# Edge terms of every fourth batch of edge_attr_128 computed in the count stage of the first mean layer instead of in the gated pass

## The reference

```python
x = _layernorm(x + _L0_gnn_ref(x, edge_index, edge_attr_64, ...))   # gated messages
x = _layernorm(x + _L1_gnn_ref(x, ..., src, dst))                   # mean of neighbours
x = _layernorm(x + _L2_gnn_ref(x, edge_index, edge_attr_128, ...))  # two attention layers
x = _layernorm(x + _L3_gnn_ref(x, edge_index, ...))                 # two mean layers
```

## Time and profile before

| | us |
|---|---|
| median of 3 runs | 2037.59 |
| lowest and highest run | 2037.51, 2041.03 |
| the profiled execution | 2039.3 |
| its span, first to last instruction | 2037.5 |
| gated pass, steady part, in the span | 79.41 to 642.36 |
| count stage, pairs 0 to 207 | 683.88 to 962.40 |

### The profile page before, as it was taken

How to read it: one execution, slowest core, us unless ns; L and a number is a source line. 1 busy time by engine, 2 the same in 40 slices (tenths; PEclk the granted TensorE clock), 3 DMA queues, 4 the chain that set the end, 5 groups by cost and what they waited for, 6 DMA issues and landing times. The chain is left out here.

```text
span 2037.5 us, 42968 instructions
## 1 busy us (share of the span) xinstructions
PE 1742.0 (85%) x13651; PEld 1405.7 (69%) x13651; DVE 1412.8 (69%) x4286; ACT 911.7 (45%) x2490; POOL 983.6 (48%) x998
## 2 busy tenths in 40 slices
PE   5799999999999558888466999967599999299996
PEld 5699999999998425445464878757467878166664
DVE  5687788888886778885667766655676664744656
ACT  2566667676665266664303544421154453411100
POOL 3776777777774300000356777735577775300000
PEclk9799999999999759999768999986699999699998
DMA  6988788888884011222352111107221111344542
GB/s 191 269 241 240 235 240 255 256 249 246 255 255 148 7 55 55 109 109 89 127 143 62 45 41 43 45 15 200 70 67 41 41 43 37 123 162 180 198 163 87
DMA packets 145067, 276.87 MB, mean 136 GB/s; under 512 B 28295, under 2 KB 88333, under 8 KB 141556
## 3 DMA queue, kind: packets, MB, share of 16 engines
q1 hardware_dynamic: 104526, 191.58, 29.2%
q0 software_dynamic: 35456, 79.88, 14.5%
q10 hardware_dynamic: 4854, 2.55, 0.5%
HBM read 228.82 MB, written 45.08 MB: 134 GB/s over the span
## 5 line engine op out<-in xcount | busy, mean ns | idle before, releaser
L959 POOL DMA_INDIRECT gated_rows<-p_tab,src_idx x416 | 429.7, 1033 | 176.0 <-issue 104.4
L1351 POOL DMA_INDIRECT ring<-table,src_idx x384 | 384.1, 1000 | 146.4 <-issue 93.0
L2159 PE MATMUL bank<-counts,mean_xs 128*128 128x416 bf16 (+2 forms) x1350 | 219.5, 321 | 32.0 <-DVE mean_xs L1671 32.0
L1000 PE MATMUL bank<-gated_wide_q,gated_comb 128*128 128x256 f32 x832 | 216.8, 384 | 0.0
L1157 DVE TENSOR_TENSOR gated_pre<-bank,gated_rows 128x512 f32<-128x512 f32 x208 | 142.8, 687 | 101.8 <-PE bank L1000 101.8
L2159 PEld LDWEIGHTS bank<-counts,mean_xs 128*128 128x128 bf16 x1350 | 126.2, 98 | 116.1 <-issue 34.4
L1482 ACT COPY attention_counts<-bank 128x475 f32 (+1 forms) x224 | 127.2, 568 | 176.3 <-PE bank L1506 153.4
L1517 PEld LDWEIGHTS bank<-attention_counts,h_sb 128*128 128x128 f32 x900 | 157.5, 190 | 62.3 <-ACT attention_counts L1482 3.8
L1073 ACT ACTIVATE gated_sig<-gated_pre 128x512 f32<-128x512 f32 x208 | 131.1, 630 | 154.1 <-DVE gated_pre L1157 152.0
L1517 PE MATMUL bank<-attention_counts,h_sb 128*128 128x232 f32 (+1 forms) x900 | 191.9, 341 | 2.3 <-DVE attention_counts L1574 1.7
L1506 PE MATMUL bank<-attention_wide_b,scratch 128*128 128x400 f32 x448 | 189.5, 505 | 0.0
(11 more groups left out here) (428 smaller groups left out, 4018.7 us busy)
## 6 DMA issues: line engine op xcount, KB each, us to landing
counts<-count_tabs SPq DMA_DIRECT2D x16, 2675.0 KB, 9.9
h_sb<-in_edge_attr_dram SPq DMA_DIRECT2D x51, 512.0 KB, 4.9
count_tabs<-mean_counts SPq DMA_DIRECT2D x8, 2675.0 KB, 7.8
gated_relr<-rel_rows SPq DMA_DIRECT2D x104, 128.0 KB
gated_ids<-id_rows SPq DMA_DIRECT2D x26, 512.0 KB
gated_wide_q<-q_tab SPq DMA_DIRECT2D x208, 64.0 KB
attend_hot_lo<-low_hots SPq DMA_DIRECT2D x52, 256.0 KB, 3.3
gated_ea<-in_edge_attr_dram SPq DMA_DIRECT2D x51, 256.0 KB
```

The source lines that it names most:

```text
L959: pool.indirect_dma_start(out=rows[:, q % TICKS, c, :], out_offset=None, in_=p_tab, in_offset=bass.IndirectOffsetOnAxis(ap=src_idx[:, b, j ...
L1000: mm = pe.matmul(PRE[q % 2][:, c * 2 * P:(c + 1) * 2 * P], comb[:, u, k, c, :], wide_q[:, u, c, :], start=True, stop=True)
L1351: pool.indirect_dma_start(out=rows[:, n % RING, j, :], out_offset=None, in_=table, in_offset=bass.IndirectOffsetOnAxis(ap=src_idx[:, gathe ...
L2159: mm = pe.matmul(BANKS_D[q % ND][:, 0:width], xs[l][:, m // 3, m % 3, :], counts[:, s % 2, m // 3, at:at + width], start=(m == 0), stop=(m ...
```

## The change

`LEFT` is the set of batches 1, 5, 9, ..., 101 (26 of 104). For these the gated pass no longer loads, turns, copies or multiplies edge_attr_128: `turn_ea` keeps the transpose of edge_attr_64 alone, `turn_silu` keeps silu alone, ACT's L1068 and L1079 fall away. A load of two batches of edge_attr_128 becomes one of one batch where the second is in LEFT; the number of DMAs stays.

In `mean_build` SP loads these batches into six buffers in `scratch` (the first six at the start, the others in between the stores of the tables). At pairs 61, 66, ..., 186 PE turns one batch behind `count(n)` (four transposes into bank TURN), ACT copies it behind `copy_counts(n)` (512 columns), and two pairs later PE multiplies it with `ae_v` behind `count(n+2)` (four matmuls, eight passes, two columns) into bank 7. At pair 190 ACT copies all terms into `ae`. The first turn waits until the W_self products have been taken. Pairs 61 to 186 lie in the third to eighth block. The core of the diff:

```diff
+    LEFT = range(1, NB, UN)
...
-                        for c in range(2):
-                            mm = pe.transpose(EAT[:, (1 + c) * P:(2 + c) * P], ea128[:, u, 2 * k + c, :], ident[:, :])
+                        if by_pe(b):
+                            for c in range(2):
+                                mm = pe.transpose(EAT[:, (1 + c) * P:(2 + c) * P], ea128[:, u, 2 * k + c, :], ident[:, :])
...
-                        for c in range(2):
-                            mm = pe.matmul(ST[:, 2 * (P + c):2 * (P + c) + 2], eaT[:, q % TRN, c, :], ae_v[:, :], start=True, stop=True)
+                        if by_pe(q // PAIRS):
+                            for c in range(2):
+                                mm = pe.matmul(ST[:, 2 * (P + c):2 * (P + c) + 2], eaT[:, q % TRN, c, :], ae_v[:, :], start=True, stop=True)
...
+            EA_FROM, EA_STEP = 2 * SBP + 9, 5
+            EA_AT = {EA_FROM + EA_STEP * i: i for i in range(NE)}
+            TERMS_AT = max(EA_AT) + 4
...
+                    due = [(EA_FROM + EA_STEP * (i - ER + 1), load, i) for i in range(ER, NE)] + [((s + 1) * SBP, keep, s) for s in range(NSB)]
...
+                    def place_eaT(i):
+                        act.wait_ge(ea_turned, i + 1)
+                        reach(act, ea_made, i - 1)
+                        act.copy(flat(eaT[:, i % 2, :, :]), TURN[:, :]).then_inc(eaT_ready, 1)
...
                         copy_counts(n, values)
+                        if n in EA_AT:
+                            place_eaT(EA_AT[n])
...
+                    def turn_ea(i):
+                        pe.wait_ge(ea_in[i % ER], 16 * (i // ER + 1))
+                        reach(pe, eaT_ready, i)
+                        for j in range(J):
+                            mm = pe.transpose(TURN[:, j * P:(j + 1) * P], ea128[:, i % ER, j, :], ident[:, :])
+                        mm.then_inc(ea_turned, 1)
...
+                    def multiply_ea(i):
+                        pe.wait_ge(eaT_ready, i + 1)
...
+                        for j in range(J):
+                            at = 2 * (i * J + j)
+                            mm = pe.matmul(TERMS[:, at:at + 2], eaT[:, i % 2, j, :], ae_v[:, :], start=True, stop=True)
+                        mm.then_inc(ea_made, 1)
...
                             count(n)
...
+                            if n in EA_AT:
...
+                                turn_ea(EA_AT[n])
+                            if n - 2 in EA_AT:
+                                multiply_ea(EA_AT[n - 2])
```

More of the change, by code:

```diff
@@ L161, in build_program @@
     place_a, origin_a = sb("place_a", [1, NSB * ATP], I32), sb("origin_a", [1, LAST], I32)
+    LEFT = range(1, NB, UN)
+    assert NB - 1 not in LEFT and UN == 4
     ae_v, ae = sb("ae_v", [P, 2]), sb("ae", [P, 2, NB, J])
@@ L866, in batch, with by_pe @@
                 return q // PAIRS, q % PAIRS, q // PAIRS % UN
+            def by_pe(b):
+                return b not in LEFT
             def rounds_of(engine):
@@ L1065, in place_eaT @@
                         act.copy(comb[low, u, k, 0, :], EAT[low, 0:P])
-                        act.copy(comb[high, u, k, 1, :], EAT[high, 0:P])
-                        reach(act, s_turned, q - TRN + 1)
-                        act.copy(flat(eaT[:, q % TRN, :, :]), EAT[:, P:3 * P]).then_inc(eaT_ready, 1)
+                        ins = act.copy(comb[high, u, k, 1, :], EAT[high, 0:P])
+                        if by_pe(b):
+                            reach(act, s_turned, q - TRN + 1)
+                            ins = act.copy(flat(eaT[:, q % TRN, :, :]), EAT[:, P:3 * P])
+                        ins.then_inc(eaT_ready, 1)
                     def sigmoid(q):
@@ L1686, in mean_build @@
             most, flag = sb("most", [1, 1]), sb("flag", [1, 1], I32)
+            ea128 = scratch[:, 0:ER * J * P].rearrange("p (b j d) -> p b j d", b=ER, j=J)
+            NE = len(LEFT)
+            eaT = flat(cur[:, :, :])[:, 2048:2048 + 2 * J * P].rearrange("p (u j d) -> p u j d", u=2, j=J)
             sig, cnt = h_sb, sb("cnt", [P, NT])
             BANKS_D, BANKS_C = [bank[0], bank[1]], bank[2:2 + CR]
-            TURN, ZB = bank[6], 2
+            TURN, TERMS, ZB = bank[6], bank[7], 2
+            assert 2 * J * NE <= 512 and 1024 + sum(FAR) <= 2048
             w_n = wide_w[:, P:2 * P]
@@ L1696, in mean_build @@
             normed, normed_d = sem("normed"), sem("normed_d")
+            ea_turned, eaT_ready, ea_made, ae_kept = sem("ea_turned"), sem("eaT_ready"), sem("ea_made"), sem("ae_kept")
             measured, variance, root, deviation, by_act, by_dve, rstd_ready = norm_parts("n", sb, sem)
             lo_ready, wide_ready, onto_ready, counted, copied = sem("lo_ready"), sem("wide_ready"), sem("onto_ready"), sem("counted"), sem("copied")
+            ea_in = [sem(f"ea_in{u}") for u in range(ER)]
             load_self, _, _, turn_self, copy_self, multiply_self, take_self, self_sems = self_parts(
                 sem, x_from, w_self, w_neigh, b, TURN, flat(cur[:, 0:GROUP, :]), residual=True)
+            self_taken = self_sems[3]
             cast, rest = thirds(x_from, xs, left, (cast0, cast1, rest0, rest1))
@@ L1707, in mean_build @@
             FLAG_AT, CLEAR_AT = 45, 40
-            assert 1 + max(SPLIT_AT) < SBP
+            assert 1 + max(SPLIT_AT) < SBP and max(SELF) + 3 < EA_FROM and TERMS_AT < NDD
             def by_engine(g):
@@ L1738, in _, with load @@
                 def _(sp):
+                    def load(i):
+                        reach(sp, ea_turned, i - ER + 1)
+                        sp.dma_start(ea128[:, i % ER, :, :], a["edge_attr_128"][LEFT[i] * BE:(LEFT[i] + 1) * BE, :]
+                                     .rearrange("(p j) d -> p j d", j=J)).then_inc(ea_in[i % ER], 16)
                     def keep(s):
@@ L1743, in _ @@
                     clear_spent(sp)
+                    sp.wait_ge(turned, 1)
+                    for i in range(ER):
+                        load(i)
                     sp.wait_ge(a_made, NG)
                     load_self(sp)
-                    for s in range(NSB):
-                        keep(s)
+                    due = [(EA_FROM + EA_STEP * (i - ER + 1), load, i) for i in range(ER, NE)] + [((s + 1) * SBP, keep, s) for s in range(NSB)]
+                    for _, issue, i in sorted(due, key=lambda d: d[0]):
+                        issue(i)
                     sp.wait_ge(flagged, 1)
```

22 lines of the change are left out of this document (17 added, 5 removed).

## The result

The changed kernel takes 2065.22 us (median of 4 runs, 2063.23 to 2066.59) where the kernel before, run beside it, takes 2037.84 (2037.51 to 2041.03): a ratio of 1.0123, 95% interval 1.0099 to 1.0146. It is slower by 27.4 us. The profiled execution took 2063.23 us, 23.9 more than that of before (2039.3).

What follows compares the result with a forecast made beforehand. PE was taken to limit both stages. Count stage 32.5 - 2.9 - 2.7 + 7.6 = +34.5 us, less 14.4 in the gated pass, is +20.1; on the median 2037.59 that gives 2057.7 us, range 2044 to 2069.

Steps and rivals of the forecast that it cites:

- Gated pass: Gated pass: 14.4 of PE's 30.2 us come off, mostly transposes; the multiplies' saving is mostly lost waiting in round 0.
- Rival A: Gated pass: the whole saving arrives, DVE and ACT keeping up in round 0; -29.7 + 34.5, 2042.4 us; chance 0.12.
- Rival B: Count stage: insertions vanish into PE's idle 24.5 us and beside its matmul streams; 2023.2 us; chance 0.05.
- The inserted passes: Count stage: 26 times four transposes (0.44 us) and eight multiply passes (0.81 us) on PE, 32.5 us (30.4 to 37.4).
- Waits, less what hides: Count stage: multiplies waiting for ACT's copies add 7.6 us; 2.9 hide at long loads, 2.7 come from ACT being less late.
- The place at 133: Count stage: multiply of pair 133 waits behind ACT's long load; wait grows 1.5 us, 1 us of work pushed behind it.
- Free of cost: SP's loads: Count stage: SP's edge loads, issued 25 pairs ahead, do not hold up the stores of the count tables; no cost.
- the clock behind the waits: Count stage: 1 us of work pushed behind the long wait runs partly at granted clock 0.50; not priced separately.
- Rival C: Count stage: ACT a second limit, every multiply waits about 0.5 us, clock lower more often; 2071 us; 0.11 with Rival D.
- Rival D: Gated pass: rounds don't shorten, the wait moves from round 0 to others; 34.5 alone, 2072 us; 0.11 with Rival C.

Runs made afterwards that it cites:

- experiment 5: Kernel before with only the multiplies of the 26 batches and the small copy behind them left out of the gated pass, their terms too: 2034.09 us, ratio 0.9948.
- experiment 3: Kernel before without the 26 batches' edge work in either stage (terms zero), and DVE's mask making two rounds earlier in each eight: 2007.46 us, ratio 0.9845.
- experiment 4: Kernel before with DVE's mask making two rounds earlier in each eight (round 4 instead of 6), nothing else: 2037.92 us, ratio 0.9996.
- experiment 6: Changed kernel with the 26 insertions at other pairs, none within two pairs of ACT's loads of window starts; edge loads move along: 2061.19 us, ratio 1.0089.
- experiment 9: Changed kernel with ACT's count-stage loads of window starts beginning at a multiple of four values: 2019.93 us, ratio 0.9912 to the kernel before.
- experiment 1: Kernel before with the 26 batches' edge work removed from the gated pass and not done in the count stage, terms zero: 2022.43 us, ratio 0.9916.
- experiment 8: Changed kernel with DVE's mask making two rounds earlier in each eight of the gated pass: 2050.06 us, ratio 1.0037 to the kernel before.
- experiment 10: Changed kernel with aligned count-stage loads of window starts on ACT and DVE's mask making in round 4 of eight: 2009.24 us, ratio 0.9863 to the kernel before.
- experiment 2: Kernel before with its gated pass whole, and the 26 batches' edge work done once more in the count stage: 2076.19 us, ratio 1.0191.
- experiment 7: Kernel before with ACT's count-stage loads of window starts beginning at a multiple of four values: 1999.89 us, ratio 0.9791.

## Why the prediction held, and where it was off

The forecast was 2057.7 us, slower, in a range of 2044 to 2069; 2065.2 is in it, 7.5 above the forecast. By the traces the difference is 23.9 where I had 20.1. The mechanism of each stage was right: one round in eight takes back what the multiplies save, and the inserted passes cost their full time. That the total came so near is in part luck, as the first item says.

- **Gated pass, -14.4 forecast, -13.5 measured.** The reading that only the transposes count, and that PE meets a bank that is not free in round 0, is shown by the round of 3.11 us, by experiment 5's rounds, and by experiments 3 and 4 from the other side. A group of eight gained 0.50 us (360.66 to 352.65 for 16 groups) where 0.44 + 0.04 was worked out; the groups of pairs 16 to 72, with the self transposes, 0.88 (165.83 to 159.66 for seven), which is 0.44 + 0.44; I had counted six. The first two groups gave 2.7 us (42.90 to 40.21) where some 1.3 was counted, and the end took 3.4 back: up to pair 200 the pass gained 16.9. I had let the wait at the late edge data take the gain of batch 101 alone. Of the 3.4 us the growth of that wait is 0.85; the rest goes with the low clock around it, 13.65 us instead of 6.83, which I had not priced. Other executions of the same gated code had 6.83 us there (experiments 6 and 9), took 579.5 and 579.6 us and gained 16.5 us, 10.24 in experiment 1. So that -13.5 lies so near -14.4 is luck: I counted too little for the groups, and the low clock took the excess back in this execution.
- **Rival A (all of it)** fell with the wait in round 0. It was worth 10 to 13 us more of gated time (experiments 3, 8 and 10), and experiment 3 shows what it wanted: DVE's masks two rounds earlier.
- **Rival B (room in the count stage)** fell with experiment 2: 38.4 us for work that was to be free. The 24.5 us of idle time on PE are still there (24.9). The rule of the Trainium skill that spoke for B (Perfetto Trace Analysis, Identifying the Most-Contended Engine) reads headroom from the share of peak FLOPs and from the weight loads' share, and the second was 50% there; the trace does not agree: PE had none but in the waits.
- **The inserted passes, 32.5 forecast, 32.7 measured** (experiments 7 and 9, net of small waits and of what hides). The price of eight passes, 0.81 us from the group of four in the gated pass, came out as 1.66 - 0.85 = 0.81; the other bound, 1.00 from the self product, would have been 5 us too much. The nearer row was that with the same two columns.
- **Waits, less what hides, +2.0 forecast (7.6 - 2.9 - 2.7).** The sizes of the waits at the short loads were too high: 0.10 us at pair 83 (0.6 forecast), 0.10 at 93, 0.37 at 108 (1.1), 1.39 at 158 (1.9). The place at 133 was right, and that wait grew by 2.2 us (7.51 to 9.68) where 1.5 was forecast. Over the stretch PE's idle time rose by 0.4 us; against the pair of kernels with aligned loads, the waits cost the changed kernel 1.2 us more than the kernel before (22.3 and 21.1). "Free of cost: SP's loads" did not hold as far as it goes: ACT's register loads at pairs 78 and 130 took about 1 us longer each in the three traces in which edge loads are issued beside them (experiment 6), which takes back up to 2 us of what I had counted as hidden.
- **The term that failed: the clock behind the waits.** I named it ("partly at the low clock") and gave it no price of its own but the 1 us pushed behind the wait. Between pairs 61 and 207 the time at 0.50 grew from 20.5 to 37.5 us, and PE's busy time by 38.0 us for 32.5 us of passes. By the kernels with aligned loads the low clock costs 9.4 us in the changed kernel and 5.0 in the kernel before, 4.4 more. That and the 1.2 us of waits make the 5.6 us by which the stage's 38.3 lies above 32.7. The 4.4 is a lower value, since experiment 9 itself has 3.41 us at 0.50 in this stretch and experiment 7 none. Experiment 6, which moves the insertions and the edge loads that go with them, takes 3.9 us of the clock's share away. Why the two stretches doubled stays open: one stands behind the wait that I named, the other behind a wait that was no longer than before. The Trainium skill (TensorE: Matmul & The Clock Gate, Terms) sets the penalty at the time spent throttled times the missing share of the clock: half of 17.0 us, 8.5. The trace gives 4.4: PE stands still for more than half of one of the long stretches (6.35 us busy of 13.65).
- **Rival C**, waits of 0.5 us before every multiply, did not occur; only its second part, the clock, did. **Rival D** fell with the rounds of 2.60 us.

## What to carry to other kernels

Work taken from the engine that is busy for 100% of a stretch is a gain only in the rounds where nothing else is just in time; the gap between the release of its buffer and its start, round by round, tells which they are, and the round without a gap takes the gain of the rounds ahead of it. Before work is moved into a stage with idle time, ask what the idle time is: here it was four register loads, and to shorten these (39 us in the trace) was worth more than anything the moved work could bring. An instruction that waits for a copy is badly placed where that copy is queued behind a long load, and what such a place costs is not only the wait: here the low clock cost 4.4 us more and the waits 1.2.

## What was not expected of the hardware

A TENSOR_LOAD of 26 values into ACT's registers took 10.2 us when its source began 8 bytes off a multiple of 16, and 2.7 us or less when it began at one; 28 values from an aligned start took 1.8 to 2.0 us, but for the last block's of experiments 9 and 10 (2.7 and 2.5). Of the attention pass's loads the unaligned took 3.0 (ACT) and 3.2 us (DVE), the aligned 1.0 to 1.4.

In these kernels the stretch at 1.2 GHz around a wait of 5 to 10 us came out as 6.83, 10.24 or 13.65 us. It is not the length of the wait that decides: around waits of 7.55 and 7.51 us in the kernel before it was 6.83, around one of 7.43 us in the changed kernel 13.65, and around 9.68 us 13.65 too. Nor is it the code: at the end of the gated pass the same instructions had 13.65 us (wait 5.90), 10.24 (6.22, experiment 1) and 6.83 (6.16 and 6.30, experiments 6 and 9), and the shortest and the longest differ by some 2.5 us of time. What decides it was not tested, so a forecast can only take them all.
